# Self attentions of a four-layer decoder: order of ScalarE's side evictions, how the probabilities are turned, and four products whose result is not read

## The reference

```python
q, k, v = heads(x @ Wq), heads(x @ Wk), heads(x @ Wv)
scores = einsum('bhtd,bhsd->bhts', q, k) * scale
attn = softmax(where(causal, scores, -inf))        # sa0, sa1, sa3 are causal
y = einsum('bhts,bhse->bhte', attn, v)
out = y.reshape(B, T, C) @ Wo
```

## Time and profile before

| | |
|---|---|
| median of 3 runs | 6444.49 us (6421.35 to 6450.44) |
| the profiled execution | 6416.58 us, its span 6414.8 us |
| mean granted clock of TensorE | 0.768 of full |
| TensorE busy | 4773.7 us (74%), 20662 records |
| VectorE busy | 3437.4 us (54%) |
| ScalarE busy | 2451.0 us (38%) |
| GpSimd busy | 1999.7 us (31%) |
| line 2655 (values), TensorE | 2560 records, 428.8 us |
| line 2639 (turns), TensorE | 1280 records, 246.2 us, 200.1 us idle before them |

### The profile page before, as it was taken

How to read it: one execution, slowest core, us unless ns; L and a number is a source line. 1 busy time by engine, 2 the same in 40 slices (tenths; PEclk the granted TensorE clock), 3 DMA queues, 4 the chain that set the end, 5 groups by cost and what they waited for, 6 DMA issues and landing times. The chain is left out here.

```text
span 6414.8 us, 80803 instructions
## 1 busy us (share of the span) xinstructions
PE 4773.7 (74%) x20662; PEld 3396.3 (53%) x20662; DVE 3437.4 (54%) x5067; ACT 2451.0 (38%) x3674; POOL 1999.7 (31%) x1091
## 2 busy tenths in 40 slices
PE   7889999999797876667768888888467344432598
PEld 5768888888543765346655555555256122221344
DVE  3344444444344322444446666664633999996444
ACT  2245555555222211123325555555122555550122
POOL 0045555555100001000016666665000455550000
PEclk6579999999798556765559999998655666665699
DMA  2100000000011212120112111120020000000011
GB/s 72 46 8 15 15 15 15 15 15 8 19 43 51 37 28 62 43 79 20 32 27 45 44 42 41 41 47 21 3 50 16 17 21 24 25 15 0 0 46 40
DMA packets 153360, 193.03 MB, mean 30 GB/s; under 512 B 91760, under 2 KB 136576, under 8 KB 152864
## 3 DMA queue, kind: packets, MB, share of 16 engines
q1 hardware_dynamic: 152992, 188.87, 12.1%
HBM read 134.07 MB, written 19.05 MB: 24 GB/s over the span
## 5 line engine op out<-in xcount | busy, mean ns | idle before, releaser
L1021 POOL TENSOR_TENSOR pexp_lo<-arena,pexp_hi 128x800 fp32r<-128x800 f32 x384 | 727.8, 1895 | 423.9 <-POOLq L1020 423.4
L976 POOL TENSOR_TENSOR pexp_lo<-arena,pexp_hi 128x800 fp32r<-128x800 f32 x384 | 628.4, 1637 | 504.4 <-POOLq L975 504.4
L1940 DVE TENSOR_REDUCE arena<-ps 128x1 f32<-128x482 f32 (+3 forms) x624 | 393.3, 657 | 397.3 <-DVEq L1918 382.8
L2085 DVE TENSOR_REDUCE arena<-ps 100x1 f32<-100x482 f32 (+1 forms) x768 | 477.0, 656 | 222.1 <-DVEq L2054 204.3
L1275 ACT ACTIVATE arena<-ps 128x800 f32<-128x800 f32 x384 | 322.3, 839 | 545.5 <-ACTq L1273 543.5
L1341 ACT ACTIVATE arena<-ps 128x800 f32<-128x800 f32 x384 | 321.7, 838 | 407.9 <-ACTq L1335 402.6
L2655 PEld LDWEIGHTS ps<-arena 100*100 100x100 f32 x2560 | 455.0, 283 | 17.2 <-issue 4.1
L1725 DVE TENSOR_REDUCE arena<-ps 100x8 f32<-100x800 f32 x160 | 158.7, 992 | 541.9 <-DVEq L1722 541.9
L2655 PE MATMUL ps<-arena 100*100 100x9 f32 (+1 forms) x2560 | 428.8, 312 | 2.7 <-PEq L2647 2.7
L2392 DVE MATCH_REPLACE8 arena<-arena 100x1444 f32<-100x1444 f32 x256 | 430.1, 1728 | 0.0
L3009 PE MATMUL ps<-kst,qs 96*100 96x482 f32 (+1 forms) x768 | 334.6, 437 | 116.5 <-PEq L2969 112.5
(11 more groups left out here) (356 smaller groups left out, 10539.2 us busy)
## 6 DMA issues: line engine op xcount, KB each, us to landing
ctxT<-in_ctxT SPq DMA_DIRECT2D x64, 541.5 KB
ctxk<-in_ctx SPq DMA_DIRECT2D x48, 528.0 KB
kst<-mid SPq DMA_DIRECT2D x128, 180.5 KB, 3.1
heads_dram<-arena SPq DMA_DIRECT2D x20, 800.0 KB
chunk<-in_ff_chunks SPq DMA_DIRECT2D x77, 193.0 KB, 2.4
arena<-gate_dram SPq DMA_DIRECT2D x64, 200.0 KB, 3.1
kst<-xn SPq DMA_DIRECT2D x64, 180.5 KB, 2.9
q_rows<-heads_dram SPq DMA_DIRECT2D x36, 200.0 KB
```

Of the source, the lines that this page charges most:

```text
L976: own(nc.gpsimd.tensor_tensor(pexp_lo[p % 3][:, :, :], pexp[p % 3], pexp_hi[p % 3][:, :, :], ALU.subtract))
L1021: own(nc.gpsimd.tensor_tensor(pexp2_lo[p % 3][:, :, :], pexp2[p % 3], pexp2_hi[p % 3][:, :, :], ALU.subtract))
L1940: peak = nc.vector.tensor_reduce(mparts[0:at.stop - at.start, m, c:c + 1], bank(k, z - a, at.stop - at.start), AX.X, ALU.max)
L2085: peak = nc.vector.tensor_reduce(mparts2[:, h, c:c + 1], bank(k, z - a, S), AX.X, ALU.max)
```

## The change

Three edits, all in the loop of the self attentions. ScalarE's side evictions of step k move from behind the copies of step k to behind the exponential of step k + 1, ahead of its copies; `root` moves from behind the copies of step 2 to behind the exponential of step 2. TensorE's `turn` first waits for the copies of the step before, then issues four bf16 products of 100 x 100 by 400 columns to banks 4 and 5, whose result nobody reads (the turns overwrite it), and then waits for the exponential. The eight transposes of a step become eight ordinary fp32 products by the identity.

```diff
@@ ScalarE
+            def sides(k, u, par, first, last):
+                if k in VALUES_AT[nsm] and not last:
+                    i = VALUES_AT[nsm].index(k)
+                    value_rows(1 - par, i, 4 * (u + 1) + i if cfg.get("gate") else None)
+                if not first and k in TURNS_AT[nsm]:
+                    features(k - TURNS_AT[nsm][0])
+
             def unit(u, par, first=False, last=False):
                 for k in range(8):
...
                                          scale=float(cfg["scale"])).then_inc(s.probs_ready, 1)
+                    if not first and k == 2 and cfg.get("diff"):
+                        root()
+                    if k > 0:
+                        sides(k - 1, u, par, first, last)
+                    elif not first:
+                        sides(7, u - 1, 1 - par, u == 1, False)
                     for c in range(2):
...
                                              ACT.Copy).then_inc(s.probsT_ready, 1)
-                    if k in VALUES_AT[nsm] and not last:
-                        i = VALUES_AT[nsm].index(k)
-                        value_rows(1 - par, i, 4 * (u + 1) + i if cfg.get("gate") else None)
-                    if not first and k == 2 and cfg.get("diff"):
-                        root()
-                    if not first and k in TURNS_AT[nsm]:
-                        features(k - TURNS_AT[nsm][0])
@@ TensorE
+            def unread(n):
+                for i in range(n):
+                    mm(bank(4 + i % 2, GT, S), ident_bf[0:S, 0:S], causal_bf[:, :], start=True, stop=True)
+
             def turn(k, first):
-                pe.wait_ge(s.probs_ready, 1)
-                pe.sem_inc(s.probs_ready, -1)
                 if not first:
                     pe.wait_ge(s.probsT_ready, 2)
                     pe.sem_inc(s.probsT_ready, -2)
+                unread(4)
+                pe.wait_ge(s.probs_ready, 1)
+                pe.sem_inc(s.probs_ready, -1)
                 for c in range(2):
                     for j in range(4):
                         at = c * GT + j * S
-                        last = nc.tensor.transpose(bank(4 + c, S, S, j * S), probs[:, k % 2, at:at + S], ident[0:S, 0:S])
+                        last = mm(bank(4 + c, S, S, j * S), probs[:, k % 2, at:at + S], ident[0:S, 0:S], start=True, stop=True)
                     last.then_inc(s.turned, 1)
```

## The result

The changed kernel takes 6178.74 us (median of 4 runs, 6157.35 to 6208.25), the kernel before, in the runs beside it, 6432.92. The ratio is 0.9609, 95% interval [0.9556, 0.9662]: faster by 3.9%. The forecast was 6223 us, in a range of 6100 to 6410. The profiled execution is the slowest of the four: 6208.25 us, its span 6206.5.

A forecast was written before the change was run, and what follows sets the result against it. TensorE at 1.2 GHz was taken to bound the four loops (1038.3 us). All steps high gave minus 328, low steps plus 122: 6416.6 - 206 = 6211, raised to 6223 for the median; range 6100 to 6410.

The forecast's parts named there:

- What bounds the kernel: Self-attention loops: TensorE at 1.2 GHz bounds plain steps, 5.33 us each; side evictions ahead of the exponential lengthen others.
- The prices at either clock: TensorE's step at 2.4 GHz: unread 0.68, turn 1.4, scores 0.67, values 1.43, together 4.2 us; 8.0 at 1.2 GHz.
- rival (c): TensorE's turns: an ordinary fp32 turn costs four transposes, not two; 211 us more, about 6430 us; chance 0.04.
- The clock: The four loops: 5.34 us gap-free at the low clock raises it after most low steps; PEclk 0.8 or more, sa2 about 0.7.
- a twelfth: Share of sa1's steps taken to run at the low clock, costing 10 us.
- the fifth: Share of sa0's and sa3's steps taken as low, for value rows with one-row bias products: 12 x 3.8 = 47 us.
- the sum: All loops: minus 328 us with every step high, plus 122 for low steps, so minus 206: 6211 us like the profiled execution.
- What is late next: After the change: TensorE still bounds the steps, root stays a stall, and bank 7's wait is the narrow place.
- Bank 7: TensorE's wait for bank 7 at line 2647: counted as 0, with 0.3 us a step as the bad end.
- this edit alone: ScalarE's side evictions moved behind the next exponential: about 145 us saved at the low clock, bounds 0 and 188.

The follow-up runs named there:

- e1: The kernel before with only ScalarE's new order (side evictions and root moved); turns stay transposes, no unread products: 6246.11 us, ratio 0.968.
- e8: The changed kernel with turns as transposes again and eight unread products in place of four: 6104.43 us, ratio 0.947 to the kernel before.
- e6: The changed kernel without the one-row product that adds the values' bias in sa0 and sa3: 6145.16 us, ratio 0.9532 to the kernel before.
- e5: The changed kernel with VectorE's scaling in sa2 put behind the shift of step 3: 6125.48 us, ratio 0.9519 to the kernel before.
- e9: The changed kernel with transposes, eight unread products and sa2's scaling behind the shift of step 3: 6101.8 us, ratio 0.9461 to the kernel before.
- e11: The changed kernel with transposes, eight unread products in sa0 and sa3, six in sa1 and sa2, sa2's scaling behind step 3's shift: 6109.68 us, ratio 0.9471.
- e10: The changed kernel with transposes, six unread products and sa2's scaling behind the shift of step 3: 6110.63 us, ratio 0.947 to the kernel before.

## Why the prediction was right

**What bounds the kernel.** Right. TensorE at 1.2 GHz bound the plain steps, and side evictions ahead of the exponential stretched the others; e1 shows both, with the steps of 5.25 us untouched and those with value rows at 6.53.

**The prices at either clock.** Unread 0.70 (forecast 0.68), turns 1.41 (1.4), scores 0.71 (0.67; a product of the scores is of type float32r and takes one record, not the two of other fp32 products), values 1.43; a step 4.17 us (4.2) and in sa2 3.83 (3.85). At the low clock four unread products took 1.34 (1.33) and the turns 2.57 in sa2 (2821.03 to 2823.60 in its timeline) and 2.66 behind the stall (forecast 2.67). The product turn, which the trace before did not have, cost twice the transpose, 1.41 us against 0.69 in e8, both at the high clock: rival (c), with the factor of four from the Trainium skill's section Terms ("TensorE: Matmul & The Clock Gate"), is out.

**The clock.** It rose, and where. Forecast loops of 170, 149, 170 and 350 us, measured 163, 135, 163 and 351. The low share of sa1 was 0.02, not a twelfth, and this is most of the difference; in sa0 and sa3 it was 0.3 of the time, by steps about the fifth that I had taken (a low step is nearly twice as long). That the one-row products do it was a guess then; e6 shows it. For sa2 PEclk 0.79 against about 0.7 forecast; this 0.7 was a slip, since 19 low steps of 7.25 us are 0.39 of 350 us, a PEclk of 0.8. The number of low steps was my choice and not derived, so that sa2 came out at 351 us where I had 350 is in part luck. So is the sum: an execution like the profiled one was to take 6211 and the profiled one took 6208, but the loops came out 20 us below their forecast and the rest of the span, which I had unchanged, 18 us above.

**What is late next.** `root`: 4.3 to 4.9 us of idle in each of seven units where I had 4, with one to three low steps behind each. Bank 7: 0.3 us of waiting in the whole run, so the 0 was right for this kernel. It was the next narrow place all the same: once `root`'s stall was shortened, e5 waited 5.5 us there and e9 14.9.

**The mis-sized term.** "So this edit alone is worth about 145 us at the low clock": 203. By loops it brought 33, 38 and 28 us in the causal ones where I had 22 each, and 96 in sa2 where I had 80. I charged all 31 or 63 intervals of a loop with a full step of TensorE, but the first are short (3.05 and 4.02 us between exponentials in sa0 of e1, where TensorE's first step has no values), value rows cost 1.28 and 0.51 us where I had 1.4 and 0.7, and practically all the idle time before turns went (200 us before, 26 in e1). The final sum was made on the whole step at both clocks and not on this term, so only the full count of steps reached it: sa1 was to take 139 us with every step high, and took 135. But the error hid that the clock edits bring only about 50 of the 254 us, and a loss in sa2.

## What to carry to other kernels

Before anything is done for the clock, take away the waits: behind the waits of 4.3 us at `root` the clock fell each time, behind the waits of about 1 us in e5 in six units of seven, and with the old order the same clock edits were worth nothing (0.9992), with the new one 0.7% and, better chosen, 2%. A side operation belongs behind the next instruction that another engine waits for, not ahead of it. If products are added only to hold the clock, let them have many rows and let nothing real be made dearer for it: cheap bf16 products held it better than dearer turns, and each stage is to be judged by its own time and clock (sa2 lost 28 us by the clock edits). When a stall is taken out, look for the wait behind it: in e9 bank 7 took back more than half of what had been freed at `root`.

## What the runs showed of the hardware

- Rows matter for TensorE's clock, not only gap-free issue: the same four products on 1 row in place of 100 left PEclk at 0.57 in sa1 (0.99 with 100 rows), and leaving 12 one-row products out of sa0 took it from 0.84 to 0.98.
- Transposes in a step did not keep the clock from being high nearly all the time (PEclk 0.96, 0.93 and 0.92 in sa0 in three kernels with eight of them and eight bf16 products in a step).
- A stage outside of the change ran at one of two paces. The windows of the batches of the second layer's cross attention, from the first to the last record of its transposed maxima, in the kernel before:

```profile
2333.10:2591.80 258.70, 163.12 (x867) 131.47 (x867) 56.93 (x132) 30.32 (x76) 24.41 (x30) 0.68 0.26 60
```

in the changed kernel:

```profile
2225.60:2505.00 279.40, 183.89 (x866) 147.61 (x867) 56.92 (x132) 30.32 (x76) 24.46 (x30) 0.59 0.25 56
```

and in e11:

```profile
2190.70:2450.50 259.80, 164.15 (x867) 131.99 (x867) 56.91 (x132) 30.27 (x76) 24.41 (x30) 0.68 0.26 60
```

The instructions are the same, 15 intervals of 17.2 or of 18.6 us each, and the clock is 0.68 or 0.59. These 21 us are more than the 18 by which the rest of the changed kernel's span is longer, and in the fourteen profiles of this study the stretch between sa1 and sa2 took either 549 to 556 us or 575 to 582. Kernels that hardly differ show either (e8 and e9 took 577 and 576 us, e10 and e11 549 and 553). What chooses between them, and whether one kernel shows both, is not shown, since each kernel has one profile. So a difference of some 20 us between two profiled executions need not come from the stage under study.
